# Plain attentions: one ScalarE exponential over two PSUM banks, both freed by one signal

## Chip, cores and metric

One core of a Trainium2 chip runs the whole program. The time is device microseconds of one execution; lower is better. The kernel before was run three times: 3387.08 us median, 3380.86 to 3398.59 us.

## What is computed (the reference, cut to what matters here)

Eight layers over 32 sequences of 128 tokens with 128 features, each added to the residual stream: four cross-attention blocks and four mixture-of-experts blocks. Every attention has 16 heads of size 8. The part that matters is the softmax attention, which in the reference reads, for each head:

```python
scores = jnp.einsum('bhqd,bhkd->bhqk', qh, kh) / jnp.sqrt(jnp.float32(DK))
scores = jnp.where(causal, scores, jnp.float32(-jnp.inf))   # some layers: no mask, or a window of 64
attn = jax.nn.softmax(scores, axis=-1)
ctx = jnp.einsum('bhqk,bhkd->bhqd', attn, vh)
```

There are five such "plain" attentions: L0, L1, two in L2 (L2a causal, L2b over the context) and L3. A sixth user of the exponential, the gated mixture of attentions in L2's feed-forward part (E), works on other shapes and is not changed.

## The kernel before, in words

**Work and order.** The 32 sequences form two streams of 16, each worked off in 8 pairs of sequences. The program of each engine is one straight line of instructions. It is written as a Python generator per stream, and one planner (`choose_order`, L150) merges the two streams, using a cost and a delay written beside each step of TensorE's generator; all engines follow that one merged order (`follow`). So while one stream's pair is in an attention, TensorE does steps of the other stream between its steps: another attention, tiles of a mixture (`mixture`), or units of the gated attention. The numbers of the planner do not depend on what is changed here.

**PSUM.** The eight banks (128 x 512 f32 each, allocated one by one at L191) are shared by both streams and all steps through rings (L69): `RINGS = {"t": (0, 1, 2, 3), "s1": (0, 1), "s2": (2, 3), "g": (4, 5, 6, 7)}`. `Banks.fill` (L140) hands out the next bank of a ring and counts its uses. Each bank has a semaphore `filled` (TensorE has finished it) and `taken` (its reader has finished it). `open_bank` (L346) makes TensorE wait until the bank's last use is taken; `taken` (L355) makes TensorE wait for the reader's result. A wait for a value that was already waited for is not issued again (`w.new`).

**A plain attention**, per pair of sequences and for each sequence b of the two. Heads are in four bands of four heads; a band is one bank.

- `scores` (L418): TensorE computes q k for each band into a bank of ring "g" and DVE takes the row maxima (L1594).
- `scores_t(b)` (L436): TensorE opens all four banks of ring "t" (banks 0 to 3) at once, computes the transposed scores of the four bands (L443), adds the mask where there is one (L447), and then, band by band, subtracts the maxima with four small matmuls a band (L453) and signals the band as filled.
- ScalarE's `exps(b)` (L1138) runs `exp` (L1125, the ACTIVATE is at L1130) once a band: it waits for the band's bank, writes 128 x 512 exponentials to `ex` in SBUF, and signals the bank as taken. With two sequences, 16 pairs and five attentions this is 160 runs of four.
- `weigh(b)` (L458): TensorE multiplies `ex` by the values (L463), band by band; before each band it waits for that band's exponentials. ScalarE copies the result (oT, L1089), and TensorE turns it (L472).

After `scores_t(b)`, steps of the other stream may stand ahead of `weigh(b)` in TensorE's program. Those that use banks 0 to 3 are: `scores_t` of the other stream (all four banks, L443); in a mixture tile `first` (one of banks 0 and 1, L536) and `second` (one of banks 2 and 3, L544); in a gated unit `scores` (one of banks 0 and 1, L585) and `scores_t` (one of banks 2 and 3, L594, L598), whose exponential is also the function at L1130 (256 of its 896 calls).

```python
ps = [open_bank("t", *k, "sT", b, j) for j in range(BANDS)]                      # scores_t
for j in range(BANDS):                                                          # exps
    exp(j, last_read, *k, "sT", b, j)
```

Of the kernel before, what the change touches and what calls it, by code (L numbers as in the profile page):

```python
# [7 lines left out]
F32 = mybir.dt.float32  # L8
# [3 lines left out]
ACT = mybir.ActivationFunctionType  # L12
AX = mybir.AxisListType

P = 128
# [8 lines left out]
BANDS = 4  # L24
HB = H // BANDS
NE = 8
SCALE = float(D) ** -0.5
# [88 lines left out]
class Counts:  # L116


    def __init__(self):
        self.n, self.seen = {}, {}  # L120
# [13 lines left out]
class Banks:  # L134


    def __init__(self):
        self.turn, self.uses, self.fills = {}, [0] * 8, {}

    def fill(self, ring, key):  # L140
        n = self.turn.get(ring, 0)
        self.turn[ring] = n + 1
        i = RINGS[ring][n % len(RINGS[ring])]
        self.uses[i] += 1
        assert key not in self.fills, key
        self.fills[key] = (i, self.uses[i])
        return self.fills[key]


def choose_order(streams):  # L150
# [31 lines left out]
def build(nc, A, out, totals):  # L182
    with ExitStack() as ctx:
# [4 lines left out]
            return [sb(f"{name}{s}", shape, dt) for s in range(STREAMS)]  # L188

        sem = {n: ctx.enter_context(nc.semaphore(n)) for n in SIGNALS}  # L190
        bank = [ctx.enter_context(nc.psum_tensor(f"bank{i}", [P, 512], F32)) for i in range(8)]  # L191
        banks = Banks()


# [44 lines left out]
        ex = two("ex", [P, BANDS, HB, P])  # L239
# [97 lines left out]
        def _(pe):  # L337
            w = Counts()
# [4 lines left out]
            mm.then_inc(sem["bias_made"], 1)  # L343
            pe.wait_ge(sem["bias_in"], 1)

            def open_bank(ring, *key):  # L346
                i, n = banks.fill(ring, key)
                if w.new(f"taken{i}", n - 1):
                    pe.wait_ge(sem[f"taken{i}"], n - 1)
                return bank[i]  # L350

            def filled(mm, *key):
                mm.then_inc(sem[f"filled{banks.fills[key][0]}"], 1)

            def taken(*key):  # L355
                i, n = banks.fills[key]
                if w.new(f"taken{i}", n):
                    pe.wait_ge(sem[f"taken{i}"], n)

            def stream(s):  # L360
# [53 lines left out]
                def attend(k, mask, rot=False, tail=None):  # L414
# [21 lines left out]
                    def scores_t(b):  # L436
                        if b == 0 and rot:
                            pe.wait_ge(sem[f"split_ready{s}"], w.next(f"split_ready{s}"))
                        elif b == 0:
                            taken(*k, "q")  # L440
                        ps = [open_bank("t", *k, "sT", b, j) for j in range(BANDS)]
                        for j in range(BANDS):
                            nc.tensor.matmul(ps[j][:], kf[s][band_rows(j), seq(b)], qm[s][band_rows(j), :, seq(b)],  # L443
                                             start=True, stop=False)
                        if mask is not None:
                            for j in range(BANDS):
                                nc.tensor.matmul(ps[j][:], identb[:, 0, :], masks[:, 2 * mask + 1, :].unsqueeze(1)  # L447
                                                 .to_broadcast([P, HB, P]), start=False, stop=False)
                        for j in range(BANDS):
                            taken(*k, "s", b, j)  # L450
                            for i in range(HB):
                                h = HB * j + i
                                mm = nc.tensor.matmul(ps[j][:, i * P:(i + 1) * P],  # L453
                                                      mx[s][:, b, h:h + 1].to_broadcast([P, P]), identb[:, 1, :],
                                                      start=False, stop=i == HB - 1)
                            filled(mm, *k, "sT", b, j)
# [217 lines left out]
                for i in range(PAIRS):  # L674
# [4 lines left out]
                    k = (s, i, "L0")  # L679
# [13 lines left out]
                for i in range(PAIRS):  # L693
                    tail = (s, i - 1, "B") if i else None
                    k = (s, i, "L1")
# [82 lines left out]
        def _(sp):  # L778
# [22 lines left out]
                sp.dma_start(wf[n][:], A[n]).then_inc(sem["ffn_weights_in"], 16)  # L801

            def taken(*key):
                i, n = banks.fills[key]
                if w.new(f"taken{i}", n):
                    sp.wait_ge(sem[f"taken{i}"], n)

# [117 lines left out]
        def _(pool):  # L925
# [14 lines left out]
            def stream(s):  # L940
# [55 lines left out]
                def gated_attention(k):  # L996
                    root()
                    for n in range(3):
                        yield "router"
                    yield "gate"  # L1000
                    yield "slots"
                    yield "queries"
                    for n in range(EUNITS + 4):
                        u = n - 3
                        if 0 <= u < EUNITS:
                            i, n_filled = banks.fills[(*k, "o", u)]
                            if w.new(f"taken{i}", n_filled):
                                pool.wait_ge(sem[f"taken{i}"], n_filled)
                            nc.gpsimd.tensor_tensor(mixed[s][:, u // NB % 2, u % NB, :], weighted[s][:, u % 2, 0:P],  # L1009
                                                    weighted[s][:, u % 2, P:2 * P], ALU.add)\  # L1010
                                .then_inc(sem[f"e_summed{s}"], 1)
                        yield "gated unit"
                    root()
                    yield "out"
# [58 lines left out]
        def _(act):  # L1073
# [7 lines left out]
                return bank[i]  # L1081

            def give(ins, *key):
                ins.then_inc(sem[f"taken{banks.fills[key][0]}"], 1)

            def stream(s):
                def evacuate(dst, *key):
# [37 lines left out]
                def exp(i, last_read, *key):  # L1125

                    ps = take(*key)
                    if last_read is not None:
                        take(*last_read)
                    give(nc.scalar.activation(ex[s][:, i], ps[:].rearrange("p (i q) -> p i q", i=4),  # L1130
                                              ACT.Exp, scale=SCALE), *key)
# [4 lines left out]

                def attend(k, tail=None, last_read=None):
                    def exps(b, last_read):  # L1138
                        for j in range(BANDS):
                            exp(j, last_read, *k, "sT", b, j)  # L1140

                    yield "unit"
                    yield "unit"
                    if tail is not None:
                        gate_exp()
                    yield "unit"
                    exps(0, last_read)
                    yield "unit"
                    evacuate(oT[0][s][:], *k, "o", 0)
                    yield "unit"  # L1150
                    exps(1, (*k, "o", 0))
                    if tail is not None and tail[2] == "C":
                        gate_exp()
                    yield "unit"
                    evacuate(oT[1][s][:], *k, "o", 1)
                    yield "unit"
                    yield "unit"
# [19 lines left out]
                def mixture(k):  # L1177
                    layer = k[2]
                    for n in range(TILES + 2):
                        if n < TILES:  # L1180
                            evacuate(t_turned[s][:, n % 2, :], *k, "tT", n)
                        if 1 <= n <= TILES:
                            t = n - 1
                            ps = take(*k, "h", t)
                            to = t_hid[s][:, t % 2, :]
                            if layer == 0:
                                give(nc.scalar.activation(to, ps[:], ACT.Relu), *k, "h", t)
                            elif layer == 1:
                                for c in range(CH):
                                    at = 512 + CH * P + c  # L1190
                                    ins = nc.scalar.activation(to[:, chunk(c)], ps[:, chunk(c)], ACT.Gelu,
                                                               bias=expert[s][:, t % SLOTS, at:at + 1])
                                give(ins, *k, "h", t)
                            else:
                                if t >= 2:
                                    i, m = banks.fills[(*k, "h", t - 2)]
                                    if w.new(f"taken{i}", m):
                                        act.wait_ge(sem[f"taken{i}"], m)
                                nc.scalar.activation(sg[s][:, t % 2, 0:CH3 * P], ps[:, 0:CH3 * P], ACT.Silu)\
                                    .then_inc(sem[f"silu_ready{s}"], 1)  # L1200
                        yield "tile"
# [128 lines left out]
        def _(dve):  # L1330
# [17 lines left out]
            def take(*key):  # L1348
                i, n = banks.fills[key]
                if w.new(f"filled{i}", n):  # L1350
                    dve.wait_ge(sem[f"filled{i}"], n)
                return bank[i]

            def give(ins, *key):
                ins.then_inc(sem[f"taken{banks.fills[key][0]}"], 1)

            def taken(*key):
                i, n = banks.fills[key]
                if w.new(f"taken{i}", n):
                    dve.wait_ge(sem[f"taken{i}"], n)  # L1360

# [622 lines left out]
```

## Time and profile before

| | |
|---|---|
| median of three runs | 3387.08 us |
| the profiled execution's own time | 3388.41 us |
| its span in the profile | 3386.6 us |
| TensorE matmul (PE) busy | 2822.5 us, 83% |
| weight load (PEld), VectorE (DVE) | 2069.5 us, 61%; 1971.3 us, 58% |
| ScalarE (ACT), GpSimd (POOL) | 1444.0 us, 43%; 635.2 us, 19% |
| mean granted clock of TensorE | 0.925 |

The profile is one execution. The span runs from the first to the last instruction; the execution's own time has 1.8 us more. PE is TensorE's matmul, PEld its weight load, which overlaps PE. L443 is line 443 of the kernel. "x4 2.06" means four neighbouring instructions of that line that together cover 2.06 us; instructions of one engine overlap a little, so this is less than the sum of their durations. What stands in brackets behind a row of a timeline is how long the engine had been idle and what released it.

### The profile page before, as it was taken

The page shows a single profiled execution, that of the slowest core. Times are in us where ns is not written, and L with a number is a line of the kernel's source. Part 1 is how long each engine was busy: PE and PEld are TensorE (multiplying, and loading weights), DVE is VectorE, ACT ScalarE, POOL GpSimd, SP SyncE. Part 2 cuts the span into 40 slices and gives each one's busy share as a digit, 9 for nine tenths or more (in the row PEclk, how much of TensorE's full clock was granted, in tenths as well). Part 3 has the DMA queues.
Part 4 walks back from the last instruction along what each step waited for, and adds up shares of the span by engine and source line. Part 5 has one row for each costly group of instructions (what it writes and reads, how often), then busy time and mean ns, then how long its engine had stood idle before and what let it go on. Part 6 is the DMA issues. An engine that isn't in the chain of part 4 may idle for free.

```text
span 3386.6 us, 63910 instructions
## 1 busy us (share of the span) xinstructions
PE 2822.5 (83%) x24218; PEld 2069.5 (61%) x24306; DVE 1971.3 (58%) x6642; ACT 1444.0 (43%) x3218; POOL 635.2 (19%) x853
## 2 busy tenths in 40 slices
PE   5888988866797988988988988988988988987962
PEld 2444766644575965756756756756756756756852
DVE  2566445467544456666666666666667666655442
ACT  1444434343575844434434434434434434435621
POOL 0122112233312011111111111111111111111043
PEclk7888998977898999999999999999999999998987
DMA  7300646400474600000000000000000000003464
GB/s 258 116 23 23 190 144 194 149 23 25 152 216 138 208 11 8 2 9 8 3 9 7 3 9 7 3 9 7 3 9 7 3 9 4 3 4 109 136 197 126
DMA packets 146511, 217.08 MB, mean 64 GB/s; under 512 B 20376, under 2 KB 99232, under 8 KB 146080
## 3 DMA queue, kind: packets, MB, share of 16 engines
q1 hardware_dynamic: 133920, 187.80, 18.3%
q0 software_dynamic: 12288, 25.19, 2.4%
q8 instruction: 196, 3.21, 0.4%
q14 instruction: 107, 0.88, 0.1%
HBM read 159.83 MB, written 53.08 MB: 63 GB/s over the span
## 4 chain that ended last, share of the span: by engine, by line
PE 56%; DVE 19%; ACT 13%; issue 4%; DMA 4%; POOL 2%; SPq 2%; POOLq 0%; DVEq 0%; ACTq 0%
PE bank L594 6%; ACT ex L1130 5%; PE bank L443 5%; PE bank L610 5%; PE bank L381 4%; DVE mx L1594 4%; PE bank L536 4%; PE bank L387 3%; PE bank L544 3%; PE bank L463 3%; PE bank L447 3%; DMA expert<-in_moe 3%; PE bank L453 3%; PE bank L426 2%; PE bank L432 2%
## 5 line engine op out<-in xcount | busy, mean ns | idle before, releaser
L1130 ACT ACTIVATE ex<-bank 128x512 f32<-128x512 f32 x896 | 483.7, 601 | 628.7 <-PE bank L453 433.1
L1594 DVE TENSOR_REDUCE mx<-bank 128x4 bf16<-128x512 f32 x640 | 408.3, 684 | 103.7 <-PE bank L432 54.5
L943 POOL TENSOR_TENSOR rstd<-vare,power 128x2 f32<-128x2 f32 x192 | 135.7, 707 | 1409.4 <-DVE vare L1387 1409.4
L536 PE MATMUL bank<-qm,expert 128*128 128x128 f32 x1872 | 257.5, 281 | 33.1 <-DMA expert<-in_moe 30.9
L1009 POOL TENSOR_TENSOR oT<-oT 128x128 f32<-128x128 f32 x256 | 118.7, 464 | 834.9 <-DVE oT L1710 834.9
L610 PE MATMUL bank<-ev,ex 128*128 128x65 f32 x2048 | 266.1, 273 | 0.4 <-ACT ex L1130 0.4
L952 POOL DMA_INDIRECT sent<-tail_tok,pos x192 | 191.3, 997 | 381.9 <-DVE pos L1522 338.3
L610 PEld LDWEIGHTS bank<-ev,ex 128*128 128x128 f32 x2048 | 257.3, 192 | 8.4 <-DVE mx L1594 2.1
L536 PEld LDWEIGHTS bank<-qm,expert 128*128 128x128 f32 x1872 | 231.6, 194 | 50.1 <-DMA expert<-in_moe 42.1
L381 PE MATMUL bank<-hT,wproj 128*128 128x256 f32 x736 | 231.1, 410 | 16.0 <-ACT hT L1093 8.3
L426 PE MATMUL bank<-km,qb 32*128 32x512 bf16 x640 | 138.0, 439 | 127.4 <-DVE mx L1594 37.1
L443 PE MATMUL bank<-qm,kf 32*128 32x512 f32 x1280 | 210.2, 715 | 29.6 <-ACT ex L1130 12.8
L544 PE MATMUL bank<-expert,hid 128*128 128x128 f32 x1560 | 215.6, 277 | 8.3 <-ACT ex L1130 3.9
L1698 DVE TENSOR_REDUCE emax<-bank 128x4 bf16<-128x512 f32 x256 | 174.9, 686 | 63.8 <-PE bank L585 62.9
L453 PEld LDWEIGHTS bank<-identb,mx 128*128 128x128 bf16 x2560 | 156.6, 100 | 86.4 <-issue 55.3
L594 PE MATMUL bank<-qm,ek 128*128 128x256 f32 x768 | 204.5, 390 | 3.3 <-ACT ex L1130 2.7
L544 PEld LDWEIGHTS bank<-expert,hid 128*128 128x128 f32 x1560 | 193.6, 192 | 12.6 <-ACT ex L1130 6.6
L1586 DVE RECIPROCAL rden<-bank 128x16 f32<-128x16 f32 x160 | 41.0, 256 | 272.8 <-PE bank L472 271.1
L463 PE MATMUL bank<-ex,vaug 128*9 128x128 f32 x5120 | 176.9, 276 | 8.5 <-DVE mx L1594 6.4
L453 PE MATMUL bank<-identb,mx 128*128 128x128 bf16 x2560 | 175.9, 223 | 9.0 <-DVE mx L1594 9.0
L372 PE MATMUL bank<-masks,identb 128*128 128x512 bf16 x648 | 169.4, 398 | 7.6 <-issue 3.3
L426 PEld LDWEIGHTS bank<-km,qb 32*128 32x128 bf16 x640 | 33.5, 93 | 204.1 <-issue 142.8
(208 smaller groups left out, 5266.6 us busy)
## 6 DMA issues: line engine op xcount, KB each, us to landing
expert<-in_moe SPq DMA_DIRECT2D x78, 578.0 KB, 4.6
expert<-in_moe SPq DMA_DIRECT2D x78, 512.0 KB, 4.4
expert<-in_moe SPq DMA_DIRECT2D x78, 384.0 KB, 3.8
sent<-zeros SPq DMA_DIRECT2D x8, 2560.0 KB, 9.1
ex<-sent SPq DMA_DIRECT2D x234, 64.0 KB, 3.3
answered<-qm SPq DMA_DIRECT2D x234, 64.0 KB, 3.9
ctxT<-ctx_kept SPq DMA_DIRECT2D x32, 128.0 KB, 2.1
wproj<-in_wproj SPq DMA_DIRECT2D x1, 3328.0 KB
```

The source lines that it names most:

```text
L381: mm = nc.tensor.matmul(ps[:, n * NT:(n + 1) * NT], W(weight), src[:], start=True, stop=True)
L426: mm = nc.tensor.matmul(ps[i][:], qb[s][r, seq(b)], km[s][r, :, seq(b)], start=True, stop=mask is None)
L443: nc.tensor.matmul(ps[j][:], kf[s][band_rows(j), seq(b)], qm[s][band_rows(j), :, seq(b)], start=True, stop=False)
L453: mm = nc.tensor.matmul(ps[j][:, i * P:(i + 1) * P], mx[s][:, b, h:h + 1].to_broadcast([P, P]), identb[:, 1, :], start=False, stop=i == HB ...
L463: mm = nc.tensor.matmul(ps[32 * i:32 * i + D + 1, j * P:(j + 1) * P], vaug[s][:, b, HB * j + i, :], ex[s][:, j, i, :], start=True, stop=True)
L536: mm = nc.tensor.matmul(ps[:, chunk(c)], expert[s][:, t % SLOTS, chunk(c)], t_turned[s][:, t % 2, :], start=True, stop=True)
L544: mm = nc.tensor.matmul(ps[:, 0:P], t_hid[s][:, t % 2, chunk(c)], expert[s][:, t % SLOTS, 512 + c * P:512 + (c + 1) * P], start=c == 0, st ...
L594: nc.tensor.matmul(out_[:, :, i, :], ek[p % 3][s][:, i, seq(b)], eq[s][p % 3][:, :, seq(b)], start=i == 0, stop=False)
L610: mm = nc.tensor.matmul(ps[:, i * (HE + 1):(i + 1) * (HE + 1)], ex[s][:, u % 4, i, :], ev[s][:, p % 2, b, i % 2, :], start=True, stop=True)
L952: nc.gpsimd.indirect_dma_start(sent[s][:], bass.IndirectOffsetOnAxis(ap=pos[s][:, i, j:j + 1], axis=0), tail_tok[s][:, j // 2, :], None).t ...
L1130: give(nc.scalar.activation(ex[s][:, i], ps[:].rearrange("p (i q) -> p i q", i=4), ACT.Exp, scale=SCALE), *key)
L1594: give(nc.vector.tensor_reduce(mx[s][:, b, HB * i:HB * i + HB], ps[:].rearrange("p (i k) -> p i k", i=HB), AX.X, ALU.max), *k, "s", b, i)
```

## The change

ScalarE takes the bands in pairs: it waits for both banks of the pair, runs one ACTIVATE of 128 x 1024 over two neighbouring banks, and gives one signal, the `taken` semaphore of the pair's first bank. The eight banks become one PSUM tensor, so that an access can span two. `Banks` keeps count of takes apart from fills, and remembers for each bank which take freed it last; TensorE's wait to reopen a bank, and every engine's wait for a result, go by that. The wait that TensorE would do for the second bank of a pair is one it has already done, so it isn't issued. The gated attention still uses `exp`, one bank at a time.

```diff
 class Banks:
     def __init__(self):
         self.turn, self.uses, self.fills = {}, [0] * 8, {}
-
-    def fill(self, ring, key):
+        self.takes, self.taken, self.last = [0] * 8, {}, [None] * 8
+
+    def fill(self, ring, key, taken_with=None):
...
-        return self.fills[key]
+        if taken_with is None:
+            self.takes[i] += 1
+            self.taken[key] = (i, self.takes[i])
+        else:
+
+            self.taken[key] = self.taken[taken_with]
+        former, self.last[i] = self.last[i], self.taken[key]
+        return i, former
...
-        bank = [ctx.enter_context(nc.psum_tensor(f"bank{i}", [P, 512], F32)) for i in range(8)]
+        psum = ctx.enter_context(nc.psum_tensor("bank", [P, 8, 512], F32))
+        bank = [psum[:, i, :] for i in range(8)]
...
-            def open_bank(ring, *key):
-                i, n = banks.fill(ring, key)
-                if w.new(f"taken{i}", n - 1):
-                    pe.wait_ge(sem[f"taken{i}"], n - 1)
+            def open_bank(ring, *key, taken_with=None):
+                i, former = banks.fill(ring, key, taken_with)
+                if former is not None and w.new(f"taken{former[0]}", former[1]):
+                    pe.wait_ge(sem[f"taken{former[0]}"], former[1])
                 return bank[i]
...
             def taken(*key):
-                i, n = banks.fills[key]
+                i, n = banks.taken[key]
...
-                        ps = [open_bank("t", *k, "sT", b, j) for j in range(BANDS)]
+                        ps = [open_bank("t", *k, "sT", b, j, taken_with=(*k, "sT", b, j - 1) if j % 2 else None)
+                              for j in range(BANDS)]
...
             def give(ins, *key):
-                ins.then_inc(sem[f"taken{banks.fills[key][0]}"], 1)
+                ins.then_inc(sem[f"taken{banks.taken[key][0]}"], 1)
...
                     def exps(b, last_read):
-                        for j in range(BANDS):
-                            exp(j, last_read, *k, "sT", b, j)
+
+                        for j in range(0, BANDS, 2):
+                            for i in range(2):
+                                take(*k, "sT", b, j + i)
+                            if last_read is not None:
+                                take(*last_read)
+                            first = banks.fills[(*k, "sT", b, j)][0]
+                            give(nc.scalar.activation(ex[s][:, j:j + 2].rearrange("p u i q -> p u (i q)"),
+                                                      psum[:, first:first + 2, :], ACT.Exp, scale=SCALE),
+                                 *k, "sT", b, j)
```

The same replacement of `banks.fills` by `banks.taken` is made in the waits of SyncE, GpSimd, ScalarE and VectorE.

## Rows read from the trace of the kernel before

**Rows 1.** The page: busy time of the engines, and the chain that ended last.

```profile
PE 2822.5 (83%) x24218; PEld 2069.5 (61%) x24306; DVE 1971.3 (58%) x6642; ACT 1444.0 (43%) x3218; POOL 635.2 (19%) x853
...
PE 56%; DVE 19%; ACT 13%; issue 4%; DMA 4%; POOL 2%; SPq 2%; POOLq 0%; DVEq 0%; ACTq 0%
```

**Rows 2.** The line L1130: durations, waits before it, who waited for it (us, times).

```profile
L1130 ACT ACTIVATE ex<-bank x896: 587/598/617, 44.8 to 3216.5; 128x512 f32<-128x512 f32 x180
...
  PE bank L453: 433.1, 161
...
  PEld bank L594: 18.8, 29
  PE bank L443: 12.8, 13
  PEld bank L463: 11.9, 38
...
  PE bank L594: 7.7, 15
  PEld bank L544: 6.6, 13
...
  PE bank L585: 3.5, 7
```

**Rows 3.** The chain that ended last, 1583 to 1588 us.

```profile
1583.78 1.58 ACT ex L1130 x3
1585.36 0.04 issue
1585.41 1.13 PE bank L594 x4
```

**Rows 4.** The chain that ended last, 1517 to 1523 us.

```profile
1519.23 2.07 ACT ex L1130 x4
1521.30 0.14 issue
```

**Rows 5.** ScalarE's groups by form: out<-in xcount | busy, mean ns | idle before.

```profile
L1130 ACT ACTIVATE ex<-bank 128x512 f32<-128x512 f32 x896 | 483.7, 601 | 628.7 <-PE bank L453 433.1 <-PE bank L598 187.6
...
L1089 ACT ACTIVATE attT<-bank 128x256 f32<-128x256 f32 x96 | 37.0, 386 | 110.5 <-PE bank L364 110.4
```

**Rows 6.** Timeline, 222 to 229 us, a run of exponentials and the weigh behind it.

```profile
224.63 1.06 PE L453 MATMUL bank<-identb,mx 128*128 128x128 bf16 x16
225.05 2.06 ACT L1130 ACTIVATE ex<-bank 128x512 f32<-128x512 f32 x4 [2.49 <-PE bank L453]
...
226.16 1.41 PE L463 MATMUL bank<-ex,vaug 128*9 128x128 f32 x32
...
227.17 0.12 PEld L463 LDWEIGHTS bank<-ex,vaug 128*9 128x9 f32 x8 [0.37 <-ACT ex L1130]
```

**Rows 7.** Timeline, 1582.5 to 1588 us, a gated unit behind a run.

```profile
1583.34 1.07 PE L453 MATMUL bank<-identb,mx 128*128 128x128 bf16 x16
1583.78 2.06 ACT L1130 ACTIVATE ex<-bank 128x512 f32<-128x512 f32 x4 [2.24 <-PE bank L453]
...
1584.92 0.40 PE L585 MATMUL bank<-ek,qm 128*128 128x256 bf16 x2 [0.51 <-ACT ex L1130]
...
1585.41 1.13 PE L594 MATMUL bank<-qm,ek 128*128 128x256 f32 x4
```

**Rows 8.** Timeline of TensorE, 1674 to 1681 us, the same with the other banks.

```profile
1677.42 0.40 PE L585 MATMUL bank<-ek,qm 128*128 128x256 bf16 x2
...
1678.88 1.13 PE L594 MATMUL bank<-qfs,ek 128*128 128x256 f32 x4 [0.63 <-ACT ex L1130]
```

**Rows 9.** Timeline of TensorE, 387 to 391 us, a mixture tile behind a run.

```profile
388.38 1.13 PE L536 MATMUL bank<-qm,expert 128*128 128x128 f32 x8
389.75 1.16 PE L544 MATMUL bank<-expert,hid 128*128 128x128 f32 x8 [0.25 <-ACT ex L1130]
```

More of the change, by code:

```diff
@@ L803, in taken @@
             def taken(*key):
-                i, n = banks.fills[key]
+                i, n = banks.taken[key]
                 if w.new(f"taken{i}", n):
@@ L1005, in gated_attention @@
                         if 0 <= u < EUNITS:
-                            i, n_filled = banks.fills[(*k, "o", u)]
-                            if w.new(f"taken{i}", n_filled):
-                                pool.wait_ge(sem[f"taken{i}"], n_filled)
+                            i, n_taken = banks.taken[(*k, "o", u)]
+                            if w.new(f"taken{i}", n_taken):
+                                pool.wait_ge(sem[f"taken{i}"], n_taken)
                             nc.gpsimd.tensor_tensor(mixed[s][:, u // NB % 2, u % NB, :], weighted[s][:, u % 2, 0:P],
@@ L1195, in mixture @@
                                 if t >= 2:
-                                    i, m = banks.fills[(*k, "h", t - 2)]
+                                    i, m = banks.taken[(*k, "h", t - 2)]
                                     if w.new(f"taken{i}", m):
@@ L1354, in give @@
             def give(ins, *key):
-                ins.then_inc(sem[f"taken{banks.fills[key][0]}"], 1)
+                ins.then_inc(sem[f"taken{banks.taken[key][0]}"], 1)
             def taken(*key):
-                i, n = banks.fills[key]
+                i, n = banks.taken[key]
                 if w.new(f"taken{i}", n):
```

## The prediction

> **What bounds the kernel now.** I read the page first. TensorE is busy 83% of the span and carries 56% of the chain that ended last; ScalarE is busy 43% and carries 13% [rows 1]. So ScalarE's throughput isn't what the kernel lacks; what counts is how soon after the fill of a bank its exponential is finished, and what TensorE does meanwhile. About 0.5% (17 us) is what a measurement of this kernel can tell from no change.
>
> Then the line L1130, in both directions. Its idle time ends 161 times with TensorE's L453, which fills the bands, 433.1 us in all [rows 2]. There are 160 runs of four exponentials, so practically each run finds ScalarE idle and waiting for the first band. In the other direction few of TensorE's waits end with an exponential: by weight loads 29 at L594, 38 at L463, 13 at L544, by matmuls 13 at L443, 15 at L594, 7 at L585 [rows 2]. Each is short (18.8 us over 29, for instance), but the chain goes through them: at 1583 us through three exponentials of a run and on to L594 0.04 us later [rows 3], at 1519 us through all four and on to the other stream's `scores_t` 0.14 us later [rows 4]. I followed the chain past all 159 runs that the timeline shows in full: 89 have their exponentials on it. A path that is on the chain and gets longer lengthens the whole by as much.
>
> **What one pair costs.** A 512-column exponential lasts 601 ns, a 256-column copy 386 ns [rows 5]: 0.84 ns a column, 0.17 us fixed. A pair of 1024 columns is so 0.17 + 0.86 = 1.03 us, an estimate from these two rows. Four singles cover 2.06 us [rows 6], so their starts are (2.06 - 0.60) / 3 = 0.487 us apart; of that 0.43 are columns and 0.057 us is what an instruction adds when they are back to back. The pair's pitch is 0.917 us. ScalarE's busy time falls by 320 x (2 x 0.60 - 1.03), some 54 us, its occupied time by 320 x 0.057, 18 us.
>
> **When the banks come free.** Call T the start of a run now. L453 fills four bands in 1.06 us with sixteen matmuls and ScalarE starts 0.42 us after its begin [rows 6]; the bands come about 0.22 us apart. Now the releases are at T+0.60, T+1.09, T+1.57 and T+2.06. After the change ScalarE starts when the second band is full, at T+0.22, and releases both banks of the first pair at T+0.22+1.03 = T+1.25, and both of the second at T+0.22+0.92+1.03 = T+2.17. So bank 0 is free 0.65 us later, bank 1 0.16, bank 2 0.60, bank 3 0.11. No bank is free sooner. TensorE starts 0.05 us after a release.
>
> **What waits for which bank.** I laid these shifts on TensorE's timeline behind all 159 runs.
>
> - A gated unit's L594 needs one of banks 2 and 3. In 14 runs it is bank 2: L585 at T+1.14 (in seven of them waiting for bank 1), L594 at T+1.63, right at the third release [rows 7]. It moves to T+2.23: 14 x 0.60 = 8.4 us. In 15 it is bank 3, and L594 waits at T+2.12 already [rows 8]: 15 x 0.11 = 1.7 us; the later L585 there (its bank is free at T+1.30, and it begins 1.08 us after L453, which is T+0.66) is swallowed by the 0.63 us that L594 waits now.
> - `weigh` behind its own run. In the example [rows 6] it begins at T+1.11 and stands before the fourth band until T+2.12; then that last fourth (0.41 us in the chain's terms, from 227.17 us to the end of the 1.41 us at 227.57) ends it. After the change it stands before the third band until T+2.23, and two fourths are left, 0.20 + 0.41 us: it ends at T+2.84 instead of T+2.52. Starts between T+0.7 and T+1.4, 32 runs, lose about this (0.29 to 0.36 us): 32 x 0.35 = 11.2 us. A `weigh` that begins after T+1.8 loses nothing, since two fourths of work cover the second pair.
> - A mixture tile's L536 needs one of banks 0 and 1. Where it begins at T+0.75 it moves to T+1.31; L544, which waits 0.25 us now [rows 9], gives part of it back: +0.31. With the like, 12 runs, some 4 us.
> - The other stream's `scores_t`, 13 runs: +0.11 for the release. But behind four waits it begins 0.14 us after the last exponential [rows 4], L594 behind one 0.04 us after [rows 3]: three waits cost 0.10 us, 0.033 us each. The change takes two of four away: +0.04 each, 0.6 us.
> - The other runs (about half) have only L472, L426, L381 or L668 behind them, which use banks 4 to 7: nothing, as long as these fill TensorE until T+2.2.
>
> Sum: 8.4 + 1.7 + 11.2 + 4.0 + 0.6 = 26 us. The chain at those places runs through the exponentials or through TensorE itself, save in some 2 us of it, which I take off.
>
> **Waits that go.** TensorE has four waits fewer in a run (two in `scores_t`, two in `weigh`). Bounds: nothing where the queue runs ahead of the array, 0.033 us each where it doesn't, 640 x 0.033 = 21 us. I take 1 us beyond the `scores_t` above, since they stand beside matmuls that are still running: near the lower end. ScalarE's waits stay four in a run. What stands behind the exponentials in ScalarE's queue (a gated unit's keys, queries) starts 0.11 us later, covered by TensorE's work where the trace shows no wait for it; if that cover were gone, 159 x 0.11 = 17 us. I take nothing, since those copies are waited for by later steps. A single PSUM tensor, the bookkeeping and the other engines' renamed waits add no instruction: nothing.
>
> **The pair's price, bounded.** No row shows an ACTIVATE of 1024 columns or over two banks. From below: its columns alone, 0.86 us, which gives T+1.94; my overlay then still comes to some 10 us, since bank 2 and the first halves are still late. From above: nothing saved, 1.20 us long at a pitch of 0.97, T+2.39: 0.22 us more at some 86 waits, 19 us on top. I take 1.03, on the line through the two lengths that the rows show.
>
> 3388.4 + 26 - 2 - 1 = 3411.4 us against the profiled execution; that one stands 1.3 us above the median, so 3410.
>
> What the Trainium skill says lies on both sides. TensorE's waits here end with exponentials while ScalarE is 43% busy [rows 1, 2], and by that my sum is a loss. Perfetto Trace Analysis, section Optimizing Scalar/DVE Operations, has grouping pay where the engine is saturated, and says that where it isn't and causes bubbles elsewhere, breaking instructions up may finish work sooner; the trace agrees as far as ScalarE's idle time goes.
>
> **Rivals.**
>
> 1. *The delays are absorbed, no measurable change.* TensorE idles 17% of the span [rows 1], and where a gated unit's next step waits for DVE or ScalarE anyway, a late L594 is made up. For: half of the runs already show no loss. Against: 89 of them are on the chain. With half of the sum gone: 3400.
> 2. *The waits on TensorE decide, faster.* Place: `scores_t` and `weigh`, 640 waits. It decides from 23 / 640 = 0.036 us a wait, exposed everywhere. At 0.06 us it takes 38 us against 24 of loss: 3373. For: the 0.10 us between the two chains [rows 3, 4]. Against: L453 and L463 are covered by running matmuls, and only 13 places show such a gap.
> 3. *Fixed cost is worth more than I think.* ScalarE would end its run sooner than now if a pair took under 0.92 us at full overlap. Against: two lengths leave 0.86 for the columns [rows 5], and ScalarE waits for the banks, not they for it [rows 2]. Even at 0.86 bank 2 is late: 3397; this is in the case of no change. Advanced Engine Details and Errata of the Trainium skill, section The Read-Write Bubble, advises tiles of 512 or 1024 elements against a bubble between instructions and says that one instruction may read several banks; by that rule the change would be a gain, and the trace agrees only on the bubble's size, 0.057 us.
> 4. *A pair over two banks is dearer.* At the upper bound 3430.
> 5. *The change doesn't take effect*: the profile would still show 896 instructions at L1130's place. The diff leaves no way to it; 3387.
>
> **Chances.** Forecast (3404 to 3424) 0.52; rival 1 with 3, 0.32; rival 2, 0.06; rival 4, 0.08; rival 5, 0.02. Slower by over 0.5% (above 3404): 0.52 + 0.08 = 0.60; within 0.5%: 0.34; faster by over 0.5%: 0.06. The range goes from 3388 (most of the absorbed cases) to 3430 (the dear pair); rival 2 and the tails of 1 and 4 stay out, some 0.16. The forecast's own range is 3404 to 3424.
>
> **What would show it.** In the profile of the changed kernel: 320 ACTIVATEs of 128x1024 of about 1.03 us, two in about 1.95 us, the first of them 0.64 us after L453's begin; 256 left at 128x512. ScalarE busy near 1390 us. L594 behind a run at 2.23 us after the old T (2.65 after L453's begin) in all 29 cases, with waits at L594 of some 26 us instead of 18.8; weight loads at L463 waiting before the third band, in sum about twice 11.9 us. If L463 and L594 move so and the time doesn't, rival 1 is right. If TensorE's idle time by "issue" falls by tens of us, rival 2. If two pairs take 2.17 us, rival 4. My sum would be wrong at its root if the first pair started at T and not at T+0.22.

## The result and the profile after

The changed kernel takes 3433.52 us (median of four runs, 3429.64 to 3436.24) against 3383.97 us before; ratio 1.0137, 95% interval 1.0105 to 1.017. A later repeat (e9) gave 1.0146 (1.0127 to 1.0164). So it is slower, by 46 to 49 us: the forecast way, at twice the forecast size, and above the forecast's range of 3404 to 3424 us.

The page of the changed kernel: engines, chain, and the group of the new exponentials.

```profile
PE 2828.0 (82%) x24218; PEld 2068.9 (60%) x24306; DVE 1972.2 (57%) x6642; ACT 1424.2 (41%) x2898; POOL 636.4 (19%) x853
...
PE 57%; DVE 18%; ACT 12%; issue 6%; DMA 4%; SPq 1%; POOL 1%; ACTq 0%; DVEq 0%; POOLq 0%
...
L1157 ACT ACTIVATE ex<-bank 128x1024 f32<-128x1024 f32 x320 | 310.2, 1021 | 475.7 <-PE bank L464 475.6
```

TensorE and VectorE have the same work as before [rows 1]. ScalarE is busy 20 us less, not 54: in the page a pair of instructions back to back counts once where they overlap, so what fell is the occupied time. An exponential of 1024 columns lasts 1.021 us where I estimated 1.03 [rows 5]. The chain has 6% "issue" instead of 4%; rival 2 had asked for less.

Who waits for the new exponentials (us, times), the answer to [rows 2]:

```profile
  PE bank L464: 496.4, 161
...
  PEld bank L474: 23.6, 57
  PEld bank L596: 19.9, 28
  PE bank L547: 19.1, 17
...
  PEld bank L605: 17.9, 28
...
  PE bank L474: 14.6, 50
```

L474 is the weigh (L463 before), L596 and L605 the gated unit (L585 and L594), L547 the mixture tile (L536). The weigh's weight loads wait twice as long as the 11.9 us before, as forecast; its matmuls wait 14.6 us, where no such wait stood on the list before (forecast loss 11.2 us). In the gated unit the wait is now shared between L596 and L605: 37.8 us of weight loads waiting instead of 27.0, some 11 us more where the forecast had 10 (it had put them all at L594). The surprise is L547: 19.1 us in 17 waits. The same line in the kernel before:

```profile
  PE bank L536: 1.4, 3
```

Behind a run, the weigh (compare [rows 6]) and the gated unit (compare [rows 7]), from the timeline of the changed kernel:

```profile
228.35 1.06 PE L464 MATMUL bank<-identb,mx 128*128 128x128 bf16 x16
...
229.05 1.94 ACT L1157 ACTIVATE ex<-bank 128x1024 f32<-128x1024 f32 x2 [2.78 <-PE bank L464]
...
230.22 0.62 PE L474 MATMUL bank<-ex,vaug 128*9 128x128 f32 x16 [0.27 <-ACT ex L1157]
...
231.04 0.62 PE L474 MATMUL bank<-ex,vaug 128*9 128x128 f32 x16 [0.20 <-ACT ex L1157]
```

```profile
1612.58 1.07 PE L464 MATMUL bank<-identb,mx 128*128 128x128 bf16 x16
1613.30 1.94 ACT L1157 ACTIVATE ex<-bank 128x1024 f32<-128x1024 f32 x2 [2.52 <-PE bank L464]
...
1614.38 0.40 PE L596 MATMUL bank<-ek,qm 128*128 128x256 bf16 x2 [0.73 <-ACT ex L1157]
...
1615.29 1.13 PE L605 MATMUL bank<-qm,ek 128*128 128x256 f32 x4 [0.51 <-ACT ex L1157]
```

With T = begin of the subtracting matmuls + 0.42, ScalarE starts at T+0.28 or T+0.30 (forecast T+0.22), the weigh's third band at T+2.27 and L605 at T+2.29 (forecast T+2.23). Over all 159 runs the median start is 0.71 us after the begin of the subtracting matmuls, where it was 0.42 before: T+0.28. The mechanism is the forecast one, 0.04 to 0.06 us later.

**Where the time came in.** TensorE executes the same matmuls in the same order in all these kernels, so its steps can be laid side by side. This table, worked out from the timelines, gives how many us later than in the first trace of before the step at t begins:

```
t (us, before)                            400    800   1000   1150   1300   3000    end
changed kernel                            3.9    6.5   17.8   26.6   26.5   44.8   46.0
changed kernel, repeated (e9)             3.2    8.5   17.6   25.1   24.8   43.4   43.0
pair with one wait (e1)                   3.1    3.3    8.7   10.3    8.4   26.7   24.3
singles, one signal a pair (e4)           4.8    1.7    3.9    4.8    0.8   21.8   16.8
before, one more wait (e7)               -3.3   -1.3    6.3   11.3   11.7   18.1   15.8
before, again (e5)                       -0.9   -0.9   -0.8   -0.6   -1.1    2.4   -3.2
```

Against it I hold my overlay: the release shifts of the prediction, laid on TensorE's timeline of before. Between 1300 and 3000 us (gated units) the loss is 18 us, alike with one wait or two; the overlay has 13. But 20 us come in between 800 and 1150 us, where the overlay has about 5, and there the kernel with one wait has 7. Of the 20 us, 8 are more matmul time for the same matmuls, at a granted clock of 0.87 in this stretch instead of 0.90; 12 are idle time. In that stretch one stream is in the mixture with Gelu and the other in the attention L1. One place of it, before and after:

```profile
921.59 1.28 ACT L1130 ACT_TABLE_LOAD   x1
...
922.70 1.07 PE L453 MATMUL bank<-identb,mx 128*128 128x128 bf16 x16
923.13 2.06 ACT L1130 ACTIVATE ex<-bank 128x512 f32<-128x512 f32 x4 [0.26 <-PE bank L453]
...
924.36 1.13 PE L536 MATMUL bank<-qm,expert 128*128 128x128 f32 x8 [0.48 <-ACT ex L1130]
```

```profile
932.29 1.07 PE L464 MATMUL bank<-identb,mx 128*128 128x128 bf16 x16
933.00 1.28 ACT L1157 ACT_TABLE_LOAD   x1 [1.83 <-PE bank L464]
...
934.29 1.94 ACT L1157 ACTIVATE ex<-bank 128x1024 f32<-128x1024 f32 x2
...
935.46 1.13 PE L547 MATMUL bank<-qm,expert 128*128 128x128 f32 x8 [1.98 <-ACT ex L1157]
```

After a Gelu the exponential needs its table back, a load of 1.28 us. Before, it ran as soon as ScalarE had finished the Gelu, while TensorE was still computing scores. After, it begins when the second band is full, so the exponential starts 2.00 us after the begin of the subtracting matmuls instead of 0.43: 1.28 us of this are the load, the rest is the start of every pair. TensorE stands 1.98 us at L547 where it stood 0.48. The groups of loads say how often, first in the kernel before and then in the changed one:

```profile
L1130 ACT ACT_TABLE_LOAD x35 | 44.9, 1283 | 0.6
```

```profile
L1141 ACT ACT_TABLE_LOAD x26 | 33.4, 1283 | 0.5
...
L1157 ACT ACT_TABLE_LOAD x9 | 11.5, 1283 | 20.8 <-PE bank L464 20.8
```

Nine loads belong to pairs, and ScalarE idles 20.8 us in front of them; the 26 in front of the gated attention's single exponentials are reached at once (0.5 us of idle time), as all 35 were before. Seven of the nine lie between 930 and 1120 us, where the 20 us came in.

### The profile page after: what moved, and what is told of

Same layout as the page of the kernel before. It is cut to its first block, busy times and chain, and to the rows that moved or that the text cites. A ratio compares the mean times of both kernels' runs of the same rounds, so it can differ in the third digit from the quotient of the medians.

```text
span 3432.6 us, 63881 instructions
## 1 busy us (share of the span) xinstructions
PE 2828.0 (82%) x24218; PEld 2068.9 (60%) x24306; DVE 1972.2 (57%) x6642; ACT 1424.2 (41%) x2898; POOL 636.4 (19%) x853
## 4 chain that ended last, share of the span: by engine, by line
PE 57%; DVE 18%; ACT 12%; issue 6%; DMA 4%; SPq 1%; POOL 1%; ACTq 0%; DVEq 0%; POOLq 0%
PE bank L454 5%; PE bank L605 5%; PE bank L621 5%; ACT ex L1157 4%; PE bank L391 4%; PE bank L547 4%; PE bank L474 4%; DVE mx L1613 4%; PE bank L397 3%; PE bank L555 3%; PE bank L464 3%; DMA expert<-in_moe 3%; PE bank L458 3%; PE bank L382 3%; PE bank L436 2%
## 5 line engine op out<-in xcount | busy, mean ns | idle before, releaser
L1157 ACT ACTIVATE ex<-bank 128x1024 f32<-128x1024 f32 x320 | 310.2, 1021 | 475.7 <-PE bank L464 475.6
L547 PE MATMUL bank<-qm,expert 128*128 128x128 f32 x1872 | 260.7, 283 | 47.7 <-DMA expert<-in_moe 26.9
L547 PEld LDWEIGHTS bank<-qm,expert 128*128 128x128 f32 x1872 | 234.7, 196 | 66.1 <-DMA expert<-in_moe 38.8
L454 PE MATMUL bank<-qm,kf 32*128 32x512 f32 x1280 | 212.7, 724 | 32.5 <-ACT ex L1157 15.5
L1141 ACT ACTIVATE ex<-bank 128x512 f32<-128x512 f32 x256 | 153.0, 598 | 199.0 <-PE bank L609 191.0
L605 PE MATMUL bank<-qm,ek 128*128 128x256 f32 x768 | 199.2, 382 | 4.1 <-ACT ex L1157 3.6
L474 PE MATMUL bank<-ex,vaug 128*9 128x128 f32 x5120 | 180.0, 278 | 21.6 <-ACT ex L1157 14.6
L382 PE MATMUL bank<-masks,identb 128*128 128x512 bf16 x648 | 181.1, 420 | 7.7 <-issue 3.5
```

The source lines that it names most:

```text
L382: nc.tensor.matmul(ps[:], identb[:, 0, :], masks[:], start=True, stop=True)
L474: mm = nc.tensor.matmul(ps[32 * i:32 * i + D + 1, j * P:(j + 1) * P], vaug[s][:, b, HB * j + i, :], ex[s][:, j, i, :], start=True, stop=True)
L547: mm = nc.tensor.matmul(ps[:, chunk(c)], expert[s][:, t % SLOTS, chunk(c)], t_turned[s][:, t % 2, :], start=True, stop=True)
L605: nc.tensor.matmul(out_[:, :, i, :], ek[p % 3][s][:, i, seq(b)], eq[s][p % 3][:, :, seq(b)], start=i == 0, stop=False)
L1157: give(nc.scalar.activation(ex[s][:, j:j + 2].rearrange("p u i q -> p u (i q)"), psum[:, first:first + 2, :], ACT.Exp, scale=SCALE), *k, " ...
```

## The experiments

Theory A: late releases as forecast, plus table loads held back by the second wait. Theory B: the releases alone cost all of it. Ratios are against the kernel before, run beside each kernel on the same chip; intervals are 95%.

**e1, the pair with one wait.** TensorE fills the banks in order, so the second bank's signal covers both.

```diff
-                            for i in range(2):
-                                take(*k, "sT", b, j + i)
+                            take(*k, "sT", b, j + 1)
```

> The changed kernel, but ScalarE waits only for the second bank of a pair (TensorE fills in order). Theory A (release times plus held table loads): the table loads go back to where they were, right behind the instruction before them, and the first pair starts 0.64 us after the begin of the subtracting matmuls instead of 0.70; what stays is the late release of banks, +23 to +28 us on before, some 3410. Theory B (the later releases alone cost all 46 us, the loads are harmless): 3430 or more.

Measured 1.0104 (1.0088 to 1.0121). Loads and a run:

```profile
L1156 ACT ACT_TABLE_LOAD x9 | 11.5, 1283 | 0.2
```

```profile
1594.89 1.07 PE L464 MATMUL bank<-identb,mx 128*128 128x128 bf16 x16
1595.55 1.94 ACT L1156 ACTIVATE ex<-bank 128x1024 f32<-128x1024 f32 x2 [2.46 <-PE bank L464]
...
1597.54 1.13 PE L605 MATMUL bank<-qm,ek 128*128 128x256 f32 x4 [0.51 <-ACT ex L1156]
```

The loads are back in their old place, the run starts at T+0.24 and L605 at T+2.23, the forecast time. TensorE's wait at the mixture tile falls from 19.1 us to

```profile
PE bank L547 <- ACT ex L1156: 6.9, 16, 0.8
```

So 12 of the 19.1 us were the held loads; the rest is the mixture term of the sum (12 runs forecast, 16 found). The loss was 35 us, above the 23 to 28 expected. I ran it again:

> The pair with one wait once more, in more rounds, to size what the releases alone cost. Between the traces of this kernel (3410.8 us span) and of the kernel before from the later job (3383.3 us) lie 27.5 us, and the overlay gave 28: theory A, the ratio is 1.008 to 1.009 and the overlay holds. Theory B: the first ratio, 1.0104 or 35 us, stands, and 7 us of it are something that the overlay doesn't have.

Measured 1.0091 (1.0074 to 1.0107), on a chip on which both kernels took some 2% longer. 28 us would be 1.0083, inside this interval and just outside the first; the 1.0104 of theory B is inside it too, so e12 doesn't decide between its two theories. By the two medians the pair with one wait costs 31 to 35 us. Its trace ends only 24 us behind the first trace of before, but that was an execution with a low granted clock, 0.925; the seven executions of before beside e1 have 0.927 to 0.938 (mean 0.935), and e1's four 0.928 to 0.930. The second trace of before (e5, clock 0.931) has 2812.5 us of matmul time and e1's 2823.2 us, for the same matmuls. So a part of e1's loss, an estimated 5 to 10 us, is matmul time at a lower clock.

**e3, two waits, but the load called early.**

```diff
+                            if j == 0:
+                                nc.scalar.activation(warm[s][:], ident[:, 0:1], ACT.Exp)
                             for i in range(2):
                                 take(*k, "sT", b, j + i)
```

`warm` is a tile of one column.

> The changed kernel with a one-column exponential of a constant ahead of the two waits of a run, which makes the table load come early. Theory A: the loads in front of the pairs are hidden again, the start stays 0.70 us after the begin of the matmuls: 3385 + 25 to 30, some 3413. Theory B: as the changed kernel or worse, 3433 and more.

Measured 1.0108 (1.009 to 1.0126), as e1. The two waits are still there; the loads in front of pairs are not held:

```profile
L1154 ACT ACT_TABLE_LOAD x9 | 11.5, 1283 | 0.2
```

The changed kernel's two ratios lie 0.0029 and 0.0038 above e3's, so the nine held loads cost 10 to 13 us. The interval of the repeat (from 1.0127) lies clear of e3's (to 1.0126), that of the first measurement doesn't; side by side in the table's way, e3 takes in 6 us between 800 and 1150 us and the changed kernel 20. The 0.06 us by which two waits delay a start are hardly to be seen between e3 and e1.

**e7, the kernel before with one more wait**, for a value reached long ago.

```diff
+                        act.wait_ge(sem["consts_set"], CONSTS)
                         for j in range(BANDS):
                             exp(j, last_read, *k, "sT", b, j)
```

> The kernel before with one more wait, for a value long reached, ahead of the first exponential of each run. Theory A (any second wait ahead of the instruction holds back the table load that belongs to it): the nine loads start only when the first band is full, TensorE waits about 1.3 us more behind each, +9 to +13 us, ratio near 1.003; the other runs start some 0.06 us later. Theory B (only the wait for the second bank holds it): no change, 1.000, and the loads stand where they were.

Measured 1.0053 (1.0034 to 1.0073), some 18 us for a wait that never has to wait, more than the 9 to 13 expected.

```profile
L1130 ACT ACT_TABLE_LOAD x35 | 44.9, 1283 | 19.7 <-PE bank L453 19.3
```

19.3 us of idle time until TensorE's L453 has come in front of the loads. So it isn't the second bank: any second wait between the instruction before and the exponential makes the load wait too. In the table 12 to 13 us come in between 800 and 1150 us, and 6 more between 1300 and 3000 us, where no load is held. Where there is no load, the extra wait makes a run start later (compare 0.42 us in [rows 6]; the medians over 159 runs are 0.42 and 0.48):

```profile
222.60 1.06 PE L453 MATMUL bank<-identb,mx 128*128 128x128 bf16 x16
...
223.09 2.06 ACT L1130 ACTIVATE ex<-bank 128x512 f32<-128x512 f32 x4 [2.55 <-PE bank L453]
```

Whether these 0.06 us a run are the 6 us isn't shown.

**e2, single exponentials behind both banks of a pair.**

```diff
                         for j in range(BANDS):
+                            if j % 2 == 0:
+                                for i in range(2):
+                                    take(*k, "sT", b, j + i)
                             exp(j, last_read, *k, "sT", b, j)
```

> The kernel before with its four single exponentials and four signals, but ScalarE waits for both banks of a pair ahead of the pair's first exponential. Theory A: the nine table loads in front of plain exponentials are held until the second bank is full, as in the changed kernel, and each run starts 0.28 us later: +12 to +20 us for the loads and some +15 for the start, 3412 to 3420. Theory B: only the later start costs, 3400 or less.

Measured 1.0144 (1.0124 to 1.0164), 49 us: more than either theory said. Its loads are held, as theory A has it:

```profile
L1130 ACT ACT_TABLE_LOAD x35 | 44.9, 1283 | 22.1 <-PE bank L453 21.6
```

Two things stand behind the rest. I had priced the later start at 15 us, but four singles (2.06 us) from T+0.28 release the last bank at T+2.34, later than two pairs (1.94 us) do. And the clock was low, as the page's first line shows:

```profile
PE 2855.7 (83%) x24218; PEld 2077.9 (61%) x24306; DVE 1971.1 (57%) x6642; ACT 1442.6 (42%) x3218; POOL 634.2 (18%) x853
```

That is 33 us more matmul time than in the first trace of before, 23 of it between the steps of 1300 and 3000 us, at a mean granted clock of 0.917; idle time is only 10 us more. The two executions of e2 with 0.923 and 0.928 were 6 to 13 us shorter than the two with 0.917. So e2 shows that late starts and held loads lose time without any pair; how much the pairing makes up of a late start can't be read from it.

**e4 and e6, the signal alone.** Four singles with their own waits, nothing starts later. In e4 each pair of banks is freed by its second exponential, in e6 only banks 2 and 3 share. The diff is e6's against the changed kernel (`open_bank` also gets its `taken_with` only for the fourth band); in e4 the `give` stands behind the inner loop, once a pair.

```diff
                         for j in range(0, BANDS, 2):
                             for i in range(2):
-                                take(*k, "sT", b, j + i)
...
+                                ps = take(*k, "sT", b, j + i)
...
+                                ins = nc.scalar.activation(ex[s][:, j + i], ps[:].rearrange("p (i q) -> p i q", i=4),
+                                                           ACT.Exp, scale=SCALE)
+                                if j == 0 or i == 1:
+                                    give(ins, *k, "sT", b, j + i)
```

> Four single exponentials as before, each with its own wait, but the two banks of a pair freed by the second one's signal. Nothing starts later, only banks 0 and 2 come free 0.49 us later. Theory A: 14 gated units of 0.49, 32 weighs of 0.20 and a few mixture tiles, +13 to +16 us: 3400; table loads as before. Theory B: releases cost twice what I priced, +25 to +30: 3412.

> Four single exponentials with their own waits; banks 0 and 1 have their own signals, only banks 2 and 3 share one, given by the last exponential. Theory A: what costs is bank 2, for which a gated unit's scores and the third band of a weigh wait; the late bank 0 is made up by the wait for bank 2 or 3 that follows. So 1.0055 to 1.008, most of the 1.0081 of the run in which both pairs share. Theory B: both pairs cost alike, 1.004.

Measured 1.0081 (1.0064 to 1.0098) for e4 and 1.0055 (1.0036 to 1.0074) for e6. TensorE's waits of e4:

```profile
PE bank L474 <- ACT ex L1156: 8.8, 27, 0.6
...
PE bank L605 <- ACT ex L1156: 8.1, 14, 0.6
PE bank L596 <- ACT ex L1156: 7.1, 14, 0.5
```

Sharing the signal, with no exponential moved, costs 27 us, where I expected 13 to 16 and the overlay gives 18. By the medians two thirds of it are in the second pair, as theory A has it; but theory B's 1.004 lies inside e6's interval too, so the split between the pairs isn't settled. Part of the excess is TensorE's clock: the trace of e4 has 13.4 us more matmul time than the first of before between the steps of 1300 and 3000 us, for the same matmuls. All four executions of e4 had a granted clock of 0.926; the seven of before beside them had 0.927 to 0.938.

**e10, all four banks freed by the last exponential.** As e4 with one `give` for the run.

> Four single exponentials with their own waits, all four banks freed by the last one's signal: the suspected cost taken further, nothing else changed. Theory A (loss is the delay of a release laid on what TensorE does behind the run): the overlay on the timeline of before, with all banks at T+2.12, gives 73 us, where it gave 18 for the run with one signal a pair: ratio 1.018 to 1.024. Theory B (TensorE's idle time swallows long delays): under 1.014.

Measured 1.0166 (1.0145 to 1.0188): 56 us and not 73. The page's first line and the waits of TensorE:

```profile
PE 2796.2 (81%) x24306; PEld 2064.1 (60%) x24306; DVE 1973.5 (57%) x6642; ACT 1445.5 (42%) x3218; POOL 636.6 (18%) x853
```

```profile
PE bank L474 <- ACT ex L1156: 47.1, 63, 1.6
...
PE bank L596 <- ACT ex L1156: 35.4, 28, 1.5
...
PE bank L547 <- ACT ex L1156: 21.4, 17, 1.6
```

The waits are there (104 us in these three), and 26 us less matmul time than in the first trace of before stand against them, at a mean granted clock of 0.936 instead of 0.925; against the second trace (2812.5 us, 0.931) it is 16 us less. So in this kernel, unlike in e4, the longer waits came with a higher clock, and part of their price was paid back; the overlay can't see either.

**e5, the kernel before again**, for its trace.

> The kernel before once more, unchanged, to have its trace from the chip that runs the others. Theory A (TensorE's clock falls at certain places because of the later releases): the matmuls of the mask stay at 0.97 us for four near 1802 us, as in the first trace. Theory B (where the clock falls depends on the execution or the chip): some stretch of the same kind is at the lower level here too, and the total is within 0.3% of the median.

One execution: 3385.19 us, span 3383.3 us. TensorE at one place of the third stage, this trace:

```profile
1800.00:1806.00 6.00, 5.66 (x18) 1.29 (x19) 5.58 (x24) 0.21 (x1) 0.55 (x1) 0.51 0.09 25
```

The changed kernel at the same program steps:

```profile
1833.00:1836.00 3.00, 3.00 (x14) 0.75 (x12) 2.83 (x10) 0.00 (x0) 0.00 (x0) 0.50 0.02 5
```

The first trace of before has a granted clock of 1.00 there. From 1833 to 1836 us the changed kernel is at the lower level (1.2 GHz, half of 2.4), behind the same two waits for VectorE (0.86 and 1.34 us) that the first trace passes at full clock; the repeat of before is at the lower level too. So theory B holds: such dips move from execution to execution, and a step of 1 or 2 us at a single place must not be read as an effect of the change. That is said of one place: the mean clocks of whole executions do differ between the kernels (below).

**e8, the kernel before, banks opened one by one.** The experiments said that TensorE pays for the moment of a release; then it should pay to ask for each bank only when it is needed.

```diff
-                        ps = [open_bank("t", *k, "sT", b, j) for j in range(BANDS)]
+                        ps = []
                         for j in range(BANDS):
+                            ps.append(open_bank("t", *k, "sT", b, j))
```

> The kernel before, but TensorE waits for each of the four banks just ahead of its first matmul and not for all four at once. Theory A (the moment of release is what TensorE waits for): in the 13 runs where the other stream's transposed scores stand behind a run of exponentials, they start at T+0.65 and not at T+2.2 and end about 0.8 us sooner: 10 us, ratio 0.997. Theory B: the time is made up by the following wait for DVE's maxima, 1.000.

Measured 0.9975 (0.9965 to 0.9986), ten runs, 8 us faster than before and the fastest kernel here. One of the places where the scores began at T+2.2 [rows 4], matmuls and then weight loads of this kernel:

```profile
1513.42 1.06 PE L454 MATMUL bank<-identb,mx 128*128 128x128 bf16 x16
...
1514.86 2.23 PE L444 MATMUL bank<-qm,kf 32*128 32x512 f32 x8
1517.02 1.07 PE L454 MATMUL bank<-identb,mx 128*128 128x128 bf16 x16
```

```profile
1514.86 0.42 PEld L444 LDWEIGHTS bank<-qm,kf 32*128 32x128 f32 x4
1515.47 0.29 PEld L444 LDWEIGHTS bank<-qm,kf 32*128 32x128 f32 x2 [0.20 <-ACT ex L1131]
1515.96 0.29 PEld L444 LDWEIGHTS bank<-qm,kf 32*128 32x128 f32 x2 [0.20 <-ACT ex L1131]
1517.01 0.90 PEld L454 LDWEIGHTS bank<-identb,mx 128*128 128x128 bf16 x16 [0.76 <-issue]
```

T is 1513.84. L444 starts at T+1.02, as soon as TensorE is through with the steps ahead, and not at T+2.2. But it covers 2.23 us where it covered 1.14: the fourth band's weights are loaded at T+2.12, and 1.05 us go by until L454. Each band uses 32 rows of the array. Before, all eight matmuls (two a band) together covered 1.14 us, so the bands ran side by side; here the last band's two alone take these 1.05 us. Laid side by side with before, the step is 1.19 us earlier in and 1.09 us later through, a gain of 0.10 us and not of 0.8. So my reason for the expected 10 us was wrong, though the ratio came out as expected; 13 places give 1.3 us, and where the other 7 us come from isn't shown.

**e11, the same with pairs and one wait.**

> The pair with one wait, and TensorE waits for the banks of a pair just ahead of their first matmul. Theory A: the 13 places behind a run win back what the single exponentials won, less 0.6 us each for the later first release: 1.0104 less some 0.001: 1.009. It does not come below 1.000, since weighs and gated units still wait. Theory B: opening one by one is worth more with pairs, under 1.007.

Measured 1.0087 (1.0067 to 1.0106): as theory A expected, and no better than e12's 1.0091.

## Why the prediction was right and wrong

**Right.** Direction and the mechanism of the late releases. The 1.03 us (1.021), the 1.95 us for two (1.94), the release at T+2.17, and the places that pay hold; between 1300 and 3000 us the overlay gives 13 us and e1 and the changed kernel lose 18. The upper bound of the pair's price did not come to bear, and of the Trainium skill the rule from Perfetto Trace Analysis, section Optimizing Scalar/DVE Operations (grouping pays on a saturated engine), pointed the right way, the one from Advanced Engine Details and Errata, section The Read-Write Bubble, did not: the bubble saved is there, 2.06 us against 1.94, but a shorter run of ScalarE didn't help while its first releases came later. (That section gives the bubble no length; the prediction's 0.057 us is the trace's alone.) Rival 1 is refuted: the delays were not absorbed.

**Wrong: "ScalarE's waits stay four in a run".** This is the step that failed, a term put at nothing. I counted waits and not how many stand in front of one instruction. Two in front of an exponential hold its table load until the second one is met. The trace of before had 35 such loads; I looked at them only as busy time. Nine stood in the way: 10 to 13 us by e3, and e7 makes the same loss in a kernel without any pair.

**Undersized: the releases.** The sum was 26 us before deductions; measured were 31 to 35 (e12, e1). TensorE's idle time (span less matmul time) grew by no more than the sum says: e1's trace has 24 us more of it than the first of before and 17 us more than the second. What the sum has no term for is TensorE's clock. Beside the kernel before, the mean granted clock of the executions was lower in e1 (0.929 against 0.935), e3 (0.930 against 0.935), e4 (0.926 against 0.935), e2 (0.921 against 0.935), e6 and e7 (0.927 and 0.930 against 0.931), e9 and e11 (both 0.927 against 0.932) and e12 (0.919 against 0.922), and higher only in e10, which waits longest (0.935 against 0.932). What such a difference is worth the two traces of one kernel show: 2822.5 us of matmul time at 0.925 and 2812.5 us at 0.931. So an estimated 5 to 10 us of the loss in e1 and e12 are matmul time at a lower clock. Why the clock is lower when the releases are late isn't shown; a smaller part of the excess may be in the 0.01 to 0.05 us by which all is later (the overlay rises by some 5 us for each 0.06 us).

**Deductions.** The 2 us for places off the chain and 1 us for waits that go were below what a measurement can tell. Rival 2 is refuted in that TensorE has fewer waits in a run in every pair kernel and none was faster; what the waits are worth by themselves no run isolates. Rival 4 came near the total (3430) by luck: the pair was not dearer.

## What to carry to other kernels

Merging two instructions pays where their engine is the one waited for. Where it is 43% busy, look at when each buffer comes free, before and after: here the first of the merged buffers came free 0.7 us later and the last one no sooner. Count the waits in front of each ScalarE instruction that may need a table (one needless wait cost 0.5% in e7): keep it at one (the later of two signals given in order by one engine is enough), or call the table with a tiny instruction before the wait. A cheap try beside it: let the filling engine ask for each bank just ahead of its use (0.9975 here).

## What the runs showed of the hardware

- With one wait ahead of an exponential, its table load (1283 ns) ran before the wait was met (0.6 us of idle time before 35 loads); with two waits, behind both (20.8 us before nine; 19.3 us in e7, where one of the two was met long before).
- An ACTIVATE over two neighbouring PSUM banks (128x1024) took 1.021 us against 0.601 for 128x512; the line through the 256 and 512 columns of [rows 5] gives 1.03, so the second bank cost nothing beyond its columns.
- A second wait ahead of an ACTIVATE delayed it by 0.06 us even when it was met long before (e7: median start 0.48 us after the subtracting matmuls' begin instead of 0.42, 159 runs). With two band waits instead of one the difference is the same (0.71 against 0.65 us).
- Matmuls of four bands of 32 rows, issued together, covered 1.14 us; issued one band after the other as their banks came free, 2.23 us (e8).
